# Transposes of gelu rows, normalised rows and ternary weights by DMA instead of TensorE

## The chip, the core and the metric

The kernel runs on one core of a Trainium2 chip. The time is that of the device, in microseconds (us), the median of several executions. The engines are PE (TensorE), DVE (VectorE), ACT (ScalarE), POOL (GpSimd) and SP (SyncE, which here only issues DMAs).

## The reference

x has 4 batches of 256 rows and 256 columns. All is computed from the normalised rows xn:

```
xn = layernorm(x)
q = xn @ Wq.T; latent = xn @ Wkv_down.T; k = latent @ Wk_up.T; v = latent @ Wv_up.T     # 16 heads of 16
att = softmax(where(band of 64 or first 4 columns, causal; q k.T / 4))
h = gelu(bitlinear(xn, w_fc))            # 256 x 1024; bitlinear: rows normalised again, quantised in the
f = bitlinear(h, w_proj)                 # forward value, weights sign(round(w / mean|w|)) * mean|w|
out = x + (att @ v) @ Wo.T + f
```

## The kernel before

One batch is one iteration b of a loop that is written out by hand: each engine's instructions stand in their order, and semaphores join them. TensorE contracts over the partition axis, so what is contracted has to lie transposed. Three things are transposed by PE into PSUM, as matmuls with an identity: the normalised rows (`transposed_rows`, L978), the gelu rows (`hidden_transposed`, L1126, 128x128 fp32 blocks, eight per tile i of 128 rows) and the ternary weights, fp16 (`first_ternary` L961, `second_ternary` L968). What is contracted in more than fp16's precision is split into a high and a low fp16 half: ACT writes the high half from PSUM (`rows_high` L453, `hidden_high` L461), DVE the low one, value less high half (`rows_low` L706, `hidden_low` L780). The two halves `gh` and `glo` are the stationary operands of `second_product` (L1136), which multiplies them by `prT`, the transposed ternary w_proj.

Most products go to a ring of three PSUM tiles of two banks each. `ORDER` lists who takes the next tile and what has to be done before it is free; `take` waits for that. Two more banks, `aux` and `acc`, are used by name: `acc` holds the second product, then the attention's numerator of half the heads, then the output product.

Iteration b works on three batches: attention scores and values of b, projections and row maxima of f = b + 1, the second product of a = b - 1. PE's order in b = 1 is: `maxima_transposed` (L1082), `hidden_transposed`(a, 1), `sink_scores` (L1093, L1097), `window_scores` 0 (L1107 to L1117), `second_product`(a, 0), `window_scores` 1, `latents`(f) (L990), `second_product`(a, 1), `window_scores` 2 and 3, `q_products` (L1004), `k_products` (L1019), `values` 0, `v_products`, `window_maxima` 0 (L1057, L1063), `values` 1, `window_maxima` 1, `fc_tile`(b, 0) (L1072), `window_maxima` 2, `fc_tile`(b, 1), `window_maxima` 3, `transposed_rows`(b + 2), `output_product` (L1172), `hidden_transposed`(b, 0). In b = 2 the two `fc_tile`s of the last batch stand in the place of `transposed_rows`. Iteration 0 computes the thresholds of the ternary weights (`weight_means` L649 to L661) and turns them.

On ACT stand the exponentials (L475), the gelu (`hidden`, L447), the copies from PSUM and `table_ahead` (L526), which loads the table of the next function. DVE has the row maxima (L748), reciprocals (L786), low halves and the statistics of the hidden rows (`hidden_stats`, L771, L775) and of the next rows (`row_stats` L689, `row_norm` L701). POOL computes the factors of the rows and adds the residual. SP loads `xres` (L279) and stores the result (L282, L285).

## Time and profile before

| | |
|---|---|
| median of 3 runs | 146.12 us (145.68 to 147.16) |
| profiled execution | 145.57 us, span 143.0 us |
| PE, DVE, ACT, POOL busy | 134.5, 101.1, 86.1, 29.7 us |
| HBM read, written | 6.23 MB, 1.05 MB |

The span is the time from the first to the last recorded instruction of the core; the execution's own time is longer. Busy is the union of an engine's instructions. A matmul's duration includes its way through the array, so neighbours overlap: the time that a piece of PE's work costs is read from the chain, in which each piece ends where the next begins.

### The profile page before, as it was taken

How to read it: one execution, taken by the hardware profiler on the slowest of the kernel's cores; microseconds unless marked ns; L12 is line 12 of the kernel's file. 1: busy time of each engine (PE TensorE's matmuls, PEld its weight loads, DVE VectorE, ACT ScalarE, POOL GpSimd, SP SyncE). 2: the span in 40 equal slices, each digit the busy share in tenths (PEclk: the TensorE clock that was granted, in tenths of full speed). 3: DMA queues.
4: the chain of work that ended last, by engine and by line, in shares of the span. 5: the costliest groups of instructions: out<-in, count | busy, mean ns of one | idle time of the engine just before them, and what ended most of it. 6: DMA issues, size and time to landing. Idle time of an engine off the chain costs nothing.

```text
span 143.0 us, 5152 instructions
## 1 busy us (share of the span) xinstructions
PE 134.5 (94%) x2264; PEld 103.8 (73%) x2264; DVE 101.1 (71%) x188; ACT 86.1 (60%) x128; POOL 29.7 (21%) x65
## 2 busy tenths in 40 slices
PE   7787799899999989999999999999999999999991
PEld 7575566789875477888875488888764477898981
DVE  0559999866999984952696979601969806963992
ACT  2499699498543599347542697457073479659020
POOL 8770510003500000049300000317000000025500
PEclk9999999999999999999999999999999999999999
DMA  3999720200000003000310000000400000000222
GB/s 119 309 318 371 190 72 0 77 3 7 0 5 5 0 0 78 0 5 0 95 61 0 5 0 0 7 5 0 151 5 0 0 2 5 0 5 0 76 75 73
DMA packets 7985, 7.59 MB, mean 53 GB/s; under 512 B 2580, under 2 KB 7608, under 8 KB 7864
## 3 DMA queue, kind: packets, MB, share of 16 engines
q1 hardware_dynamic: 6524, 5.90, 13.8%
q10 hardware_dynamic: 1440, 1.38, 3.2%
q8 instruction: 17, 0.28, 0.8%
q14 instruction: 4, 0.03, 0.1%
HBM read 6.23 MB, written 1.05 MB: 51 GB/s over the span
## 4 chain that ended last, share of the span: by engine, by line
PE 62%; DVE 10%; issue 1%; POOL 1%; DVEq 0%
PE acc L1136 8%; PE ring L1072 8%; PE ring L1126 5%; PE ring L1117 5%; PE acc L1162 4%; PE aux L1162 4%; PE ring L1004 4%; PE ring L1109 3%; PE acc L1172 3%; PE ring L1057 3%; PE ring L1136 3%; DVE mx L748 2%; DVE rden L786 2%; PE acc L1154 2%; PE ring L1063 2%; PE aux L1097 2%
## 5 line engine op out<-in xcount | busy, mean ns | idle before, releaser
L475 ACT ACTIVATE E<-ring,un 128x1024 f32<-128x1024 f32 x16 | 17.8, 1115 | 12.8 <-PE ring L1117 12.7
L748 DVE TENSOR_REDUCE mx<-ring 128x8 f32<-128x1024 f32 x16 | 19.4, 1220 | 2.8 <-PE ring L1063 2.6
L335 POOL TENSOR_SCALAR veh<-mvh 128x2 f32<-128x2 f32 x4 | 0.9, 218 | 71.6 <-DVE mvh L775 71.5
L447 ACT ACTIVATE gl<-ring,a 128x1024 f32<-128x1024 f32 x8 | 8.9, 1111 | 10.9 <-PE ring L1072 10.9
L780 DVE SCALAR_TENSOR_TENSOR glo<-ring,gam_r,gh 128x1024 f16<-128x1024 f32 x8 | 10.1, 1264 | 5.5 <-ACT gh L461 5.5
L716 DVE SCALAR_TENSOR_TENSOR Q<-qh,rowlo,ring 128x1024 f16<-128x1024 f16 x4 | 5.1, 1280 | 9.8 <-ACT qh L488 9.7
L1004 PE MATMUL ring<-xhT,wqT 128*128 128x256 f16 x64 | 10.3, 273 | 0.8 <-DVE wqT L624 0.8
L1136 PE MATMUL acc<-prT,gh 128*128 128x256 f16 x48 | 10.8, 274 | 0.0
L1136 PE MATMUL acc<-prT,glo 128*128 128x256 f16 x48 | 10.8, 272 | 0.0
L771 DVE BATCH_NORM_STATS2 sth<-gl 128x6 f32<-128x512 f32 x16 | 10.1, 675 | 0.0
L498 ACT ACTIVATE V<-ring 128x768 f32<-128x768 f32 x4 | 3.2, 811 | 10.7 <-PE ring L1045 10.7
L1117 PE MATMUL ring<-Q,KH 32*128 32x64 f16 (+1 forms) x192 | 9.6, 199 | 0.0
L1072 PE MATMUL ring<-fcT,xhT 128*128 128x512 f16 x32 | 9.6, 381 | 0.0
L1057 PE MATMUL ring<-mask,idb 128*128 128x512 bf16 x32 | 9.6, 380 | 0.0
L1072 PE MATMUL ring<-fcT,xlT 128*128 128x512 f16 x32 | 9.5, 379 | 0.0
L1109 PE MATMUL ring<-mov,bias 100*128 100x192 bf16 x64 | 9.3, 246 | 0.0
L1117 PE MATMUL ring<-Q,KL 32*128 32x64 f16 (+1 forms) x192 | 9.0, 197 | 0.0
L461 ACT ACTIVATE gh<-ring,gam_r 128x1024 f16<-128x1024 f32 x8 | 8.8, 1120 | 0.3 <-PE ring L1126 0.2
L1117 PEld LDWEIGHTS ring<-Q,KH 32*128 32x128 f16 x192 | 7.7, 93 | 1.7
L1063 PEld LDWEIGHTS ring<-KH,Q 32*64 32x64 f16 (+1 forms) x192 | 3.8, 100 | 6.8 <-issue 6.8
L1126 PE MATMUL ring<-idf,gl 128*128 128x128 f32 x64 | 8.6, 277 | 0.0
L1107 PE MATMUL ring<-mov,bias 100*128 100x64 bf16 x64 | 8.5, 194 | 0.0
(199 smaller groups left out, 366.9 us busy)
## 6 DMA issues: line engine op xcount, KB each, us to landing
wfc_r<-in_L_ffn_w_fc SPq DMA_DIRECT2D x1, 1024.0 KB, 6.9
wpr_r<-in_L_ffn_w_proj SPq DMA_DIRECT2D x1, 1024.0 KB, 7.4
xres<-in_L_attn_x SPq DMA_DIRECT2D x4, 256.0 KB, 4.0
bias<-in_c_bias SPq DMA_DIRECT2D x1, 825.0 KB
xin<-in_L_attn_x ACTq DMA_DIRECT2D x3, 256.0 KB, 3.2
out<-ob SPq DMA_DIRECT2D x3, 256.0 KB, 3.4
xin<-in_L_attn_x SPq DMA_DIRECT2D x1, 256.0 KB, 3.4
wq_r<-in_L_attn_Wq ACTq DMA_DIRECT2D x1, 256.0 KB, 3.8
```

The lines of the kernel that those rows point to most:

```text
L475: nc.scalar.activation(E[:, 2 * gp:2 * gp + 2, 2 * tp:2 * tp + 2, :].rearrange("p g t q -> p g (t q)"), slot("p2", b, r)[:], ACT.Exp, scal ...
L748: nc.vector.tensor_reduce(out=mx[:, i, 8 * gp:8 * gp + 8], in_=slot("f_p1", f, r)[:].rearrange("p a (t k) -> p (a t) k", t=NT), axis=AX.X, ...
L771: nc.vector.bn_stats(sth[:, i, j, :], gl[:, b % 2, i, 512 * j:512 * j + 512]).then_inc(sth_ok[0], 1)
L780: nc.vector.scalar_tensor_tensor(out=glo[:, i].rearrange("p k n -> p (k n)"), in0=flat(slot("t2T", b, i)), scalar=gam_r[:, 0:1], in1=gh[:, ...
L1004: last = nc.tensor.matmul(s[:, t // 2, (t % 2) * T:(t % 2 + 1) * T], wqT[:, w_half, c, G * t:G * t + G].rearrange("p h d e -> p (h d e)"), ...
L1057: nc.tensor.matmul(s[:, a, :].rearrange("p (t k) -> p t k", t=NT), idb[:], (mask0, mask1)[i][:].unsqueeze(1).to_broadcast([P, NT, P]), sta ...
L1072: last = nc.tensor.matmul(s[:, n, :], src[:, b % 2, c, i * P:(i + 1) * P], fcT[:, c, 512 * n:512 * n + 512], start=(m == 0), stop=(m == 2 ...
L1109: nc.tensor.matmul(s[:, a, T * j + BLK:T * j + T], bias[:, H + hm, :], mov[:, BLK:T], start=False, stop=False, skip_group_check=True)
L1117: last = nc.tensor.matmul(s[:, a, T * j + q0:T * j + q0 + n], K[g:g + 32, t, k0:k0 + P], Q[g:g + 32, t, q0:q0 + n], start=False, stop=True ...
L1126: last = nc.tensor.transpose(s[:, k // 4, (k % 4) * P:(k % 4 + 1) * P], gl[:, b % 2, i, k * P:(k + 1) * P], idf[:])
L1136: last = nc.tensor.matmul(o, src[:, i, k, :], prT[:, k, :], start=((i == 0 or b == B - 1) and k == 0 and src is gh), stop=(k == FC - 1 and ...
L1162: last = nc.tensor.matmul((acc, aux)[c][32 * k:32 * k + 32, part * T + q0:part * T + q0 + m], w.rearrange("p a d -> p (a d)"), E[:, g, t, ...
```

## The change

The three transposes leave PE, but for the rows of batch 0. A DMA transpose takes fp16 alone, so the halves are now split before they are turned: ACT and DVE write `xh`, `xl`, `gh` and `glo` from SBUF in the row layout, and SP issues `dma_start_transpose` for each: two per half of the normalised rows, one per half of a gelu tile, one per weight. PE waits for their semaphores: `xT_ok` in `latents`, `gT_ok` in `second_product`, `fcT_ok` and `prT_ok`. `hidden_high`(b, 0) follows its gelu at once. The rows are turned two iterations ahead, so `xhT` and `xlT` have three buffers. The layouts of `fcT` and `prT` follow what the DMA writes, and the moving operand of their products has two or four pieces of 128 columns. `second_product` moves behind `window_scores` 2 and 3; `latents`(f) moves to the iteration's start and from `aux` to the ring, in iteration 0 behind `window_scores` 3; `values` 1 moves behind `window_maxima` 1. On DVE `latents_low`(1) stands behind `second_ternary`, and `latents_low`(f) ahead of `hidden_low`. On POOL `second_scale` comes after the row factors. `xres` and `out` are issued behind the transposes.

```diff
--- before.py
+++ after.py
...
-        fcT = sb("fcT", [P, CC, F], fp16)
-        prT = sb("prT", [P, FC, C], fp16)
+        fcT = sb("fcT", [P, FC, CC, P], fp16)
+        prT = sb("prT", [P, CC, FC, P], fp16)
...
+        xh = sb("xh", [P, TT_, C], fp16)
+        xl = sb("xl", [P, TT_, C], fp16)
+        xhT = sb("xhT", [P, 3, CC, T], fp16)
+        xlT = sb("xlT", [P, 3, CC, T], fp16)
...
+            ORDER += [("lat", f, 0, [(latl_ok, f, 2)])] if 0 < b and f < B else []
+            ORDER += score_slots(b, range(4))
+            if f < B:
+                ORDER += projection_slots(f) + maxima_slot(f, 0) + maxima_slot(f, 1) + maxima_slot(f, 2)
+                ORDER += fc_slot(b, 0) + maxima_slot(f, 3) + fc_slot(b, 1)
+                ORDER += fc_slot(f, 0) + fc_slot(f, 1) if f == B - 1 else []
...
+            def rows_turned(n):
+                wait(sp, mm_q, n - 3)
+                wait(sp, fc, n - 3)
+                for ok, src, dst in ((xh_ok, xh, xhT), (xl_ok, xl, xlT)):
+                    wait(sp, ok, n - 1)
+                    for i in range(TT_):
+                        sp.dma_start_transpose(dst[:, n % 3, :, i * P:(i + 1) * P], src[:, i, :]).then_inc(xT_ok[0], 16)
+            def hidden_turned(b, i):
+                wait(sp, pr, b - 1, i + 1)
+                wait(sp, gh_ok, b, i + 1)
+                sp.dma_start_transpose(ghT[:, i], gh[:, i, :]).then_inc(gT_ok[i][0], 16)
+                wait(sp, glo_ok, b, i + 1)
+                sp.dma_start_transpose(gloT[:, i], glo[:, i, :]).then_inc(gT_ok[i][0], 16)
+            def first_turned():
+                sp.wait_ge(w_tern, 1)
+                sp.dma_start_transpose(fcT[:].rearrange("p k c n -> p (k c) n"), tern[:, 0]).then_inc(fcT_ok, 16)
+            def second_turned():
+                sp.wait_ge(w_tern, 1 + CC)
+                sp.dma_start_transpose(prT[:].rearrange("p c k n -> p (c k) n"), tern[:, 1]).then_inc(prT_ok, 16)
             for b in range(B):
+                if b:
+                    hidden_turned(b - 1, 0)
+                    hidden_turned(b - 1, 1)
+                else:
+                    first_turned()
+                    rows_turned(1)
+                    second_turned()
+                if b + 2 < B:
+                    rows_turned(b + 2)
+                if b == B - 1:
+                    hidden_turned(b, 0)
+                    hidden_turned(b, 1)
                 wait(sp, xa_ok, b - 1)
                 sp.dma_start(xres[:], x_v[b]).then_inc(ld_res[0], 16)
-                if b + 1 < B:
-                    wait(sp, o_ok, b)
-                    sp.dma_start(out_v[b], ob[:]).then_inc(st_out[0], 16)
+                if b:
+                    wait(sp, o_ok, b - 1)
+                    sp.dma_start(out_v[b - 1], ob[:]).then_inc(st_out[0], 16)
...
+                if b:
+                    second_scale(b - 1)
...
+            def rows_high(n):
+                wait(act, xn_ok, n)
+                wait(act, xT_ok, n - 2)
+                nc.scalar.activation(xh[:], xn[:], ACT.Copy).then_inc(xh_ok[0], 1)
...
+                wait(act, gT_ok[i], b - 1)
+                nc.scalar.activation(gh[:, i, :], gl[:, b % 2, i, :], ACT.Copy, scale=gam_r[:, 0:1]).then_inc(gh_ok[0], 1)
...
-                if b:
-                    hidden_high(a, 1)
+                if 0 < b and f < B:
+                    latents_high(f)
...
                 exponentials(b, 1)
-                if 0 < b and f < B:
-                    latents_high(f)
                 exponentials(b, 2)
-                if b == 0:
-                    latents_high(1)
+                if 0 < b and b + 2 < B:
+                    rows_high(b + 2)
...
                     hidden_high(b, 0)
+                exponentials(b, 3)
                 if b:
                     ffn_scaled(a, 0)
                     ffn_scaled(a, 1)
-                exponentials(b, 3)
                 if f < B:
                     if b == 0:
-                        first_transposed()
+                        latents_high(1)
+                        rows_high(2)
                     queries_high(f)
...
                     attended_high(b, 0)
+                    attended_high(b, 1)
                     hidden(b, 0)
-                    attended_high(b, 1)
+                    hidden_high(b, 0)
                     hidden(b, 1)
...
-                    if b + 2 < B:
-                        table_ahead(b, ACT.Exp)
-                        rows_high(b + 2)
-                    if b == 0:
-                        second_transposed()
+                    table_ahead(b, ACT.Exp)
                     attended(b)
-                    hidden_high(b, 0)
-                    if f == B - 1:
-                        table_ahead(b, ACT.Exp)
+                    hidden_high(b, 1)
...
                 wait(dve, gh_ok, b, i + 1)
-                nc.vector.scalar_tensor_tensor(out=glo[:, i].rearrange("p k n -> p (k n)"), in0=flat(slot("t2T", b, i)), scalar=gam_r[:, 0:1],
-                                               in1=gh[:, i].rearrange("p k n -> p (k n)"), op0=ALU.mult, op1=ALU.subtract).then_inc(glo_ok[0], 1)
+                wait(dve, gT_ok[i], b - 1)
+                nc.vector.scalar_tensor_tensor(out=glo[:, i, :], in0=gl[:, b % 2, i, :], scalar=gam_r[:, 0:1],
+                                               in1=gh[:, i, :], op0=ALU.mult, op1=ALU.subtract).then_inc(glo_ok[0], 1)
...
-                if 0 < b and f < B:
-                    rows_low(f)
                 maxima_moved(b)
                 if b:
+                    if f < B:
+                        latents_low(f)
                     hidden_low(a, 0)
+                    if b + 2 < B:
+                        row_stats(b + 2)
+                    hidden_low(a, 1)
+                    if b + 2 < B:
+                        row_norm(b + 2)
                     hidden_stats(a, 0)
-                    hidden_low(a, 1)
                     hidden_stats(a, 1)
+                    if b + 2 < B:
+                        rows_low(b + 2)
                 else:
                     row_norm(1)
                     weight_means(0)
                     first_ternary()
                     rows_low(1)
                     weight_means(1)
-                if f < B:
-                    latents_low(f)
-                if b + 2 < B:
-                    row_stats(b + 2)
-                    row_norm(b + 2)
-                if b == 0:
+                    row_stats(2)
+                    row_norm(2)
                     second_ternary()
+                    latents_low(1)
+                    rows_low(2)
...
+                wait(pe, xT_ok, f - 1)
+                if f == 1:
+                    wait(pe, exs, 0)
+                o = take("lat", f)[:, 0, 0:T] if f > 1 else aux[:, 0:T]
...
-            def hidden_transposed(b, i):
-                s = take("t2T", b, i)
-                wait(pe, gelu, b, i + 1)
-                for k in range(FC):
-                    last = nc.tensor.transpose(s[:, k // 4, (k % 4) * P:(k % 4 + 1) * P], gl[:, b % 2, i, k * P:(k + 1) * P], idf[:])
-                last.then_inc(tr_h[0], 1)
...
+                wait(pe, gT_ok[i], b)
+                pe.wait_ge(prT_ok, 16)
...
-                    for src in (gh, glo):
-                        last = nc.tensor.matmul(o, src[:, i, k, :], prT[:, k, :], start=((i == 0 or b == B - 1) and k == 0 and src is gh),
-                                                stop=(k == FC - 1 and src is glo), skip_group_check=True)
+                    for src in (ghT, gloT):
+                        last = nc.tensor.matmul(o.rearrange("p (c n) -> p c n", n=P), src[:, i, k, :], prT[:, :, k, :],
...
-                if b:
-                    hidden_transposed(a, 1)
+                if 0 < b and f < B:
+                    latents(f)
                 sink_scores(b)
                 window_scores(b, 0)
+                if b == 0:
+                    weight_totals(1)
+                window_scores(b, 1)
+                window_scores(b, 2)
                 if b:
                     second_product(a, 0, acc[:, 0:C])
-                else:
-                    transposed_rows(1)
-                    weight_totals(1)
-                window_scores(b, 1)
+                window_scores(b, 3)
                 if b:
-                    if f < B:
-                        latents(f)
                     second_product(a, 1, acc[:, C:2 * C])
-                window_scores(b, 2)
-                if b == 0:
-                    latents(1)
                 if f < B:
-                    window_scores(b, 3)
                     if b == 0:
-                        first_ternary()
+                        latents(1)
                     q_products(f)
                     k_products(f)
                     values(b, 0)
                     v_products(f)
                     window_maxima(f, 0)
+                    window_maxima(f, 1)
                     values(b, 1)
-                    window_maxima(f, 1)
+                    window_maxima(f, 2)
                     fc_tile(b, 0)
-                    window_maxima(f, 2)
+                    window_maxima(f, 3)
                     fc_tile(b, 1)
-                    window_maxima(f, 3)
-                    if b + 2 < B:
-                        transposed_rows(b + 2)
-                    else:
+                    if f == B - 1:
                         fc_tile(f, 0)
-                    if b == 0:
-                        second_ternary()
-                    if f == B - 1:
                         fc_tile(f, 1)
                     output_product(b)
-                    hidden_transposed(b, 0)
                 else:
-                    hidden_transposed(b, 0)
...
```

How the instructions stand at three places that the prediction speaks of. PE, from the end of iteration 0 into iteration 1, before (L1172 is `output_product`, L1126 `hidden_transposed`, L1082 `maxima_transposed`, L1093 and L1097 the first part of `sink_scores`):

```order
L1172 MATMUL acc<-woT,yhT 128x256 x4
L1172 MATMUL acc<-woT,ylT 128x256 x2
L1126 MATMUL ring<-idf,gl 128x128 x8
L1082 MATMUL aux<-idb,mhl 32x128 x2
L1126 MATMUL ring<-idf,gl 128x128 x8
L1093 MATMUL aux<-mov,bias 64x256 x2
L1097 MATMUL aux<-Q,BDH 64x256 x2
```

and now, with the line numbers of the changed kernel (L1180, L1097, then L1005 `latents`):

```order
L1180 MATMUL acc<-woT,yhT 128x256 x4
L1180 MATMUL acc<-woT,ylT 128x256 x2
L1097 MATMUL aux<-idb,mhl 32x128 x2
L1005 MATMUL ring<-xhT,wkvT 128x256 x4
L1005 MATMUL ring<-xlT,wkvT 128x256 x2
L1108 MATMUL aux<-mov,bias 64x256 x2
L1112 MATMUL aux<-Q,BDH 64x256 x2
```

The sixteen transposes round `maxima_transposed` are gone, and the six matmuls of `latents` stand where eight of them stood.

SP in one iteration, before and then now (from the `xres` of iteration 0 to the store of batch 0):

```order
L282 DMA out<-ob 128x2x256
L279 DMA xres<-in_L_attn_x 128x2x256
```

```order
L313 DMA xres<-in_L_attn_x 128x2x256
L287 DMA_TRANSPOSE ghT<-gh 128x8x128
L289 DMA_TRANSPOSE gloT<-glo 128x8x128
L287 DMA_TRANSPOSE ghT<-gh 128x8x128
L289 DMA_TRANSPOSE gloT<-glo 128x8x128
L281 DMA_TRANSPOSE xhT<-xh 128x2x128 x2
L281 DMA_TRANSPOSE xlT<-xl 128x2x128 x2
L313 DMA xres<-in_L_attn_x 128x2x256
L316 DMA out<-ob 128x2x256
```

Four transposes of gelu halves and four of the next rows now stand in one queue, and `xres` behind them; the second gelu tile's high half stands behind the first one's low half.

DVE at the start of iteration 1, before and then now (L765/L792 `maxima_moved`, L780/L808 `hidden_low`, L771/L798 `hidden_stats`, L711/L738 `latents_low`, L707 `row_stats`, L722 `row_norm`, L733 `rows_low`):

```order
L706 TENSOR_TENSOR xlT<-ring,xhT 128x512
L765 COPY mov<-aux 32x256
L780 SCALAR_TENSOR_TENSOR glo<-ring,gam_r,gh 128x1024
L771 BN_STATS sth<-gl 128x6 x2
L775 BN_AGGR mvh<-sth 128x2
L780 SCALAR_TENSOR_TENSOR glo<-ring,gam_r,gh 128x1024
L771 BN_STATS sth<-gl 128x6 x2
L775 BN_AGGR mvh<-sth 128x2
L711 TENSOR_TENSOR lat<-aux,lat 64x256
L712 TENSOR_TENSOR latS<-aux,latS 64x64
```

```order
L792 COPY mov<-aux 32x256
L738 TENSOR_TENSOR lat<-ring,lat 64x256
L739 TENSOR_TENSOR latS<-ring,latS 64x64
L808 SCALAR_TENSOR_TENSOR glo<-gl,gam_r,gh 128x1024
L707 BN_STATS st<-xin 128x6 x2
L711 BN_AGGR mv<-st 128x2 x2
L808 SCALAR_TENSOR_TENSOR glo<-gl,gam_r,gh 128x1024
L722 TENSOR_SCALAR xn<-xin,mv,rs 128x256 x2
L798 BN_STATS sth<-gl 128x6 x2
L802 BN_AGGR mvh<-sth 128x2
```

`latents_low` moved from behind both gelu tiles to ahead of them, and the work on the rows of batch 3 moved in between and behind.

## Rows read from the trace of the kernel before

**Rows 1.** The page's head, its part 1 and the granted clock of part 2.
```profile
span 143.0 us, 5152 instructions
PE 134.5 (94%) x2264; PEld 103.8 (73%) x2264; DVE 101.1 (71%) x188; ACT 86.1 (60%) x128; POOL 29.7 (21%) x65
...
PEclk9999999999999999999999999999999999999999
```
**Rows 2.** The chain that ended last, by time: start us, us, what; iterations 0 and 1.
```profile
53.53 0.87 PE ring L1126 x8
54.41 0.22 PE aux L1082 x2
54.62 1.02 PE ring L1126 x8
...
57.87 1.85 PE acc L1136 x16
...
65.36 2.73 PE ring L1004 x24
...
82.04 0.59 PE ring L978 x4
...
83.94 0.87 PE ring L1126 x8
84.81 0.21 PE aux L1082 x2
```
**Rows 3.** The same chain, iterations 2 and 3.
```profile
112.44 3.56 PE ring L1072 x16
...
118.19 0.21 PE aux L1082 x2
...
127.37 1.02 PE ring L1126 x8
...
130.43 0.44 PE acc L1154
```
**Rows 4.** Timeline of ACT: start us, us, engine, line, what; round an iteration's end.
```profile
65.30 0.83 ACT L514 ACTIVATE ffn<-acc,a 128x256 f32<-128x256 f32 x2
...
82.44 1.28 ACT L526 ACT_TABLE_LOAD   x1
...
84.32 0.68 ACT L519 ACTIVATE att<-acc,un 128x512 f32<-128x512 f32 x1
84.89 1.11 ACT L461 ACTIVATE gh<-ring,gam_r 128x1024 f16<-128x1024 f32 x1
```
**Rows 5.** The page's group of `hidden_low`: busy us, mean ns, idle before it.
```profile
L780 DVE SCALAR_TENSOR_TENSOR glo<-ring,gam_r,gh 128x1024 f16<-128x1024 f32 x8 | 10.1, 1264 | 5.5 <-ACT gh L461 5.5
```
**Rows 6.** Timeline of DVE in iteration 0, with the ternary weights.
```profile
27.58 2.35 DVE L667 SCALAR_TENSOR_TENSOR tern<-wfc_r,pthr,signs 128x2048 f16<-128x2048 f32 x1 [0.45 <-issue]
...
30.95 0.20 DVE L661 TENSOR_SCALAR gam<-gam 128x1 f32<-128x1 f32 x1
32.37 0.43 DVE L711 TENSOR_TENSOR lat<-aux,lat 64x256 f16<-64x256 f32 x1 [1.21 <-ACT latS L482]
...
32.97 0.75 DVE L689 BATCH_NORM_STATS2 st<-xin 128x6 f32<-128x256 f32 x2
...
38.52 0.88 DVE L682 TENSOR_SCALAR tern<-tern,tmean 128x1024 f16<-128x1024 f16 x2
```
**Rows 7.** Part 3 of the page: queue, packets, MB, share of 16 engines' span.
```profile
q1 hardware_dynamic: 6524, 5.90, 13.8%
```
**Rows 8.** The DMA view: issues, KB each, us from issue to landing.
```profile
xres<-in_L_attn_x SPq DMA_DIRECT2D x4, 256.0 KB, 4.0
...
out<-ob SPq DMA_DIRECT2D x2, 128.0 KB, 1.8
```
**Rows 9.** Timeline of SP: start us, us, what; one issue.
```profile
69.31 0.40 SPq L282 DMA_DIRECT2D out<-ob  x1
```
**Rows 10.** What PE waited for, of the longest: us in total, times, longest us.
```profile
PE ring L1004 <- DVE wqT L624: 0.8, 1, 0.8
```

More of the change, by code:

```diff
@@ L157, in layer_kernel @@
         a2 = sb("a2", [P, TT_], fp32)
-        gh = sb("gh", [P, TT_, FC, P], fp16)
-        glo = sb("glo", [P, TT_, FC, P], fp16)
+        gh = sb("gh", [P, TT_, F], fp16)
+        glo = sb("glo", [P, TT_, F], fp16)
+        ghT = sb("ghT", [P, TT_, FC, P], fp16)
+        gloT = sb("gloT", [P, TT_, FC, P], fp16)
         ring = [ctx.enter_context(nc.psum_tensor(f"ring{i}", [P, 2, 512], fp32)) for i in range(3)]
@@ L427, in weight_magnitudes @@
                                          accum_out=wsum[:, n, c:c + 1]).then_inc(w_abs[n], 1)
-            def first_transposed():
-                for c in range(CC):
-                    act.wait_ge(w_tr, 4)
-                    nc.scalar.activation(fcT[:, c, :], slot("t_fc", 0)[:, c, :].bitcast(fp16), ACT.Copy).then_inc(fcT_ok[0], 1)
-            def second_transposed():
-                for j in range(2):
-                    act.wait_ge(w_tr, 5)
-                    nc.scalar.activation(prT[:, 4 * j:4 * j + 4, :], slot("t_pr", 0)[:, j, :].bitcast(fp16).rearrange("p (k c) -> p k c", k=4),
-                                         ACT.Copy).then_inc(prT_ok[0], 1)
             def hidden(b, i):
@@ L949, in weight_totals @@
                 nc.tensor.matmul(acc[:, n * N_SUM:(n + 1) * N_SUM], ones[:], wsum[:, n, :], start=True, stop=True).then_inc(w_tot, 1)
-            def first_ternary():
-                s = take("t_fc", 0)
-                pe.wait_ge(w_tern, 1)
-                for c in range(CC):
-                    for k in range(FC):
-                        last = nc.tensor.transpose(s[:, c, :].bitcast(fp16)[:, k * P:(k + 1) * P],
-                                                   tern[:, 0, k * C + c * P:k * C + (c + 1) * P], idh[:])
-                last.then_inc(w_tr, 1)
@@ L961, in second_ternary @@
-            def second_ternary():
-                s = take("t_pr", 0)
-                pe.wait_ge(w_tern, 1 + CC)
-                for j in range(2):
-                    for k in range(4):
-                        for c in range(CC):
-                            last = nc.tensor.transpose(s[:, j, :].bitcast(fp16)[:, k * C + c * P:k * C + (c + 1) * P],
-                                                       tern[:, 1, c * F + (4 * j + k) * P:c * F + (4 * j + k + 1) * P], idh[:])
-                last.then_inc(w_tr, 1)
@@ L1067, in fc_tile @@
             def fc_tile(b, i):
-                wait(pe, fcT_ok, 0)
+                pe.wait_ge(fcT_ok, 16)
                 s = take("fc", b, i)
```

114 lines of the change are left out of this document (49 added, 65 removed).

## The prediction

> **What bounds the kernel now.** I read the page's busy shares first, then the chain that ended last, then what PE waits for, then the timelines of ACT and DVE round the seams. PE is busy 134.5 of 143.0 us, DVE 101.1 and ACT 86.1 [rows 1]. The chain says more than the share: from the end of iteration 0 to the last product it runs on PE alone, piece against piece, and the reader is to see that iteration 1 begins at 54.4, iteration 2 at 84.8 and iteration 3 at 118.2 us [rows 2, 3]: 30.4, 33.4 and 24.8 us to the span's end. So PE's work is the time, and the transposes that the change takes from PE lie on the path: 0.87 and 1.02 us for the eight `gl` blocks of a tile, 0.59 us for the rows [rows 2]. The profiled execution took 145.57 us for a span of 143.0, so 2.6 us lie round the span; the median of the runs is 0.55 us over that execution. I add 3.1 us to a span to compare it with the median.
>
> **What PE loses.** Per iteration 0.87 + 1.02 + 0.59 = 2.5 us, in iteration 3 three tiles, 3.1 us, in iteration 0 also the two ternary weights. If nothing took their place, this would be some 10 us in all. What takes their place is a transfer: a gelu tile reaches `second_product` by gelu, `hidden_high` (ACT), `hidden_low` (DVE), SP, DMA, where before DVE's result was read at once. ACT and DVE keep their instructions in number and shape. I price `hidden_high` and `hidden_low` from SBUF at what they take from PSUM, 1.11 and 1.26 us [rows 4, 5], and ACT's four copies of the weights, gone, at nothing: ACT is no bound.
>
> **The price of a transfer** is the disputed term, since this trace has no DMA transpose. I write S for the time by which one half of a tile (128 x 1024 fp16, 256 KB) holds the queue and the DMA engines, and F for what then passes until its semaphore is full. The row blocks (64 KB) take S/4, but not under an issue, 0.40 us [rows 9]; a weight (512 KB) takes 2S.
> S from below: the SP queue's packets moved 5.90 MB in 13.8% of 16 x 143.0 us [rows 7], which is 316 us of one engine, 18.7 KB per us; 256 KB over 16 engines are 16.4 KB each, 0.9 us. S from above: the same 316 us by 6524 packets are 48 ns each; cut by 128 columns, as the result's shape 128x8x128 has it, the half is 128 x 8 = 1024 pieces, 64 per engine, 3.1 us. I take 2.0, between them: pieces of 256 B are shorter than that queue's mean packet of 0.9 KB, so 48 ns is too dear, and a transpose writes in shorter runs than a copy, so 0.9 us is too cheap. F: a store of 128 KB lands 1.8 us after its issue [rows 8]; less the 0.4 of the issue that is 1.4. Upwards, a 256 KB load from HBM lands after 4.0 us [rows 8], less 0.4 and 0.9 is 2.7. I take 1.4, because nothing here is read from HBM.
> By the Trainium skill (Advanced Engine Details and Errata, X-Bar Transpose) transposing DMAs are as fast as regular ones; then S is at its lower end, which is the second rival below. The Trainium skill (VectorE: DVE Perf Modes, The three transpose paths) speaks against the change: it gives 1309 ns for one 128x128 block by DMA and 390 ns by TensorE. If blocks followed each other at that pace, an estimate from that page is 10.5 us for a half and a kernel of some 300 us. No row here shows either.
>
> **Where the wait falls.** In iteration b, ACT first loads the exp table (1.28), then `attended` (0.6), `hidden_high` of tile 1 (1.0), an `xin` issue (some 0.5, by [rows 9]) and `latents_high` (0.5, about one DVE instruction of its size); DVE adds `latents_low` (0.6), which now stands ahead of `hidden_low` of tile 0 (1.3) [rows 4 to 6]. The gelu ends about when the iteration begins, so `glo` of tile 0 is complete 6.0 us after that. PE meanwhile has 0.2 + 0.7 + 1.1 us and three `window_scores` of 1.1 to do, with half a us of waiting for a bank, and stands at `second_product` after 5.3 to 5.9 us. So nothing covers the transfer. SP issues in the written order gh0, glo0, gh1, glo1, so gh1, ready long before, queues behind glo0 and glo1 behind gh1: tile 1 is there at 6.0 + 3S + F. After it come the second product (1.8 us, [rows 2]) and the rest of the iteration. That rest is 84.81 - 65.36 = 19.45 us before, less 0.59 and 0.87 [rows 2], and an estimated 0.4 more where `fc_tile`(b, 1) now takes the bank of the third `window_maxima`, whose reduction is behind DVE's reciprocal: 18.4 us.
> - Iteration 1: 6.0 + 3S + F + 0.1 + 1.8 + 18.4 = 26.3 + 3S + F = 33.7 us at S = 2.0, F = 1.4, against 30.4. (For S under 1.4 tile 0 decides: 29.1 + S + F.)
> - Iteration 2: no `xin` issue on ACT (-0.6), two more `fc` tiles (+3.5 of the 3.56 of [rows 3]): 29.2 + 3S + F = 36.6, against 33.4.
> - Iteration 3: `glo` of tile 0 is complete after 1.9 us, for `hidden_high` of it ran an iteration earlier and no latents stand ahead; `values` waits for `ffn_scaled` (0.83 us [rows 4] and the hops between engines, 1.15), which a transpose covered before; from `values` on it is 143.0 - 130.4 = 12.6 us [rows 3]: 1.9 + 3S + F + 0.1 + 1.8 + 1.15 + 12.6 = 17.5 + 3S + F = 24.9, against 24.8. The halves of its own two tiles queue up to 1.9 + 7S + F = 17.3 us at the least, and the last is needed at 1.9 + 3S + F + 9.7 = 19.0: in time, but late if S nears 3. The last `xres` load is behind them on SP; it is needed 3 us later still.
> - Iteration 0: `first_ternary` ends at 29.9 us [rows 6]. SP then turns fcT (2S), and behind it, by the order on its queue, the four row blocks (S), and `latents`(1) waits for those: 29.9 + 3S + F + 0.1 = 37.4, where PE stood ready at 31. With latents 0.7 and 18.4 for the rest, iteration 1 begins at 49.1 + 3S + F = 56.5, against 54.4.
>
> Sum: 56.5 + 33.7 + 36.6 + 24.9 = 151.7 us of span, 154.8 by the median: **155 us**, 9 us slower. PE would be idle for 6 us once, and for 3.5 and 1 us in each of two iterations. The `ffn`, `out` and `xres` work moves back with PE but has slack. POOL's scale of the hidden rows, now behind the next rows' factors, is asked for only after `second_product`; it costs nothing.
>
> **The rivals.**
> - **Faster**, by one mechanism: the three `window_scores` ahead of `second_product` cover the transfer. Place: the first wait on the semaphore of tile 0. With S + F near zero iteration 1 begins at 53.9, for `second_ternary` now stands ahead of `latents_low`(1) on DVE and holds `k_products`: it can start 1.8 us earlier than before (rows statistics at 31.15 for 32.97), ends at 37.6 for 39.4, then 0.6 and 15.7 us [rows 6]. The iterations are then PE's own work, 29.4 and 32.2, and 23.4: 138.9, by the median 142 us. To be 1% under the runs, S + F must be under 1.5 us. Against it: the quickest transfer in the trace, half as large, lands after 1.8. For it: PE's relief is real, and the cover may be some tenths longer than I make it. 0.10.
> - **No difference**: S = 0.9, F = 1.4, a transpose at a copy's pace. 53.9 + 31.4 + 34.3 + 23.4 = 143.0 us, to the tenth the span of before: what PE gives back, the waits take; 146 us. 0.15.
> - **The queue becomes the bound**: S = 3.1 and F = 1.4 to 2.7. Iterations 59.8, 37.0, 39.9, and 1.9 + 7S + F + 6.1 = 31.1 in the last: 167.8 to 173; 171 to 176 us. For it: many short pieces. 0.20.
> - **The clock**: the granted clock is full in every slice [rows 1], and PE's longest wait on another engine's result is 0.8 us [rows 10]; now it would stand still for 3.5 to 6 us three times. If it came back at 1.2 GHz for as long as it was idle, each time half of that is lost, 13 / 2 = 6 us: 161 us. No row prices it, so it is no part of the sum. 0.13. The Trainium skill (TensorE: Matmul & The Clock Gate, Part 1) has idleness drop the engine to the lower level; by that rule this rival happens wherever the waits are as long as I forecast.
>
> **The numbers.** The forecast itself, S between 1.3 and 2.6 at full clock, has 0.42 and spans 148 to 164. A change under 1%, 1.5 us, can't be told from none. Faster by over 1%: 0.10. Within 1%: 0.15. Slower: 0.75, the forecast, the queue and the clock. The range goes from 145, which leaves out most of the first rival, to 176, the upper end of the queue's: about 0.15 is outside.
>
> **What would show it.** In the changed profile: no PE group that reads `gl`; DMA_TRANSPOSE rows on SP's queue, whose spacing for `ghT` and `gloT` is S and whose landing less that is F; the chain passing DVE `glo`, a transfer and then PE's `prT`, twice per iteration; `latents`(1) idle for some 6 us on `xT_ok`. PE's busy time some 10 us less in a longer span. S read there under 1.3 would prove the size wrong, with the formulas standing; iterations 1 and 2 shorter than 30 us with S over 1.5 would prove the mechanism wrong, for then the transfers are covered by something that I did not see.

## The result, and the profile after

The changed kernel takes 160.31 us (median of 4 runs, 159.59 to 161.24) against 145.9 us of the kernel before: a ratio of 1.098, 95% interval 1.088 to 1.109. The profiled execution has a span of 158.9 us, 15.9 more than before. In this ratio and those below, executions more than 1.5% above the fastest of their kernel are left out, in the medians they are not (five of combo_two's twelve, two of combo_late's ten, one of combo's ten).

The page's head, part 1, the granted clock by slice and the SP queue's row of part 3, to be read beside [rows 1] and [rows 7]:

```profile
span 158.9 us, 4966 instructions
PE 132.4 (83%) x2156; PEld 98.0 (62%) x2156; DVE 101.1 (64%) x188; ACT 82.4 (52%) x124; POOL 32.6 (20%) x65
...
PEclk9999999975599999956999999858999999999999
...
q1 hardware_dynamic: 30892, 11.90, 34.3%
```

TensorE has less to do, stands still for longer, and works at half clock in three places. Where the 15.9 us are shows in a cut by iteration (first `maxima_transposed` to the next; columns: stretch, its length, busy time and instructions of PE, granted clock, DMA share, GB/s). First the kernel before, then the changed one:

```profile
24.70:54.30 29.60, 28.43 (x539) 1.00 0.04 12
54.30:84.70 30.40, 30.40 (x543) 1.00 0.10 28
84.70:118.10 33.40, 33.40 (x555) 1.00 0.06 18
118.10:143.00 24.90, 22.03 (x449) 1.00 0.10 34
```
```profile
25.10:60.50 35.40, 27.25 (x491) 0.86 0.32 66
60.50:94.80 34.30, 30.73 (x522) 0.90 0.28 63
94.80:132.70 37.90, 34.20 (x540) 0.91 0.21 47
132.70:158.90 26.20, 19.52 (x425) 1.00 0.61 102
```

The iterations grew by 5.8, 3.9, 4.5 and 1.3 us. PE's idle time (length less busy) went from 4.0 to 22.1 us; its busy time fell by 2.6, although about 7.2 us of the new busy time are only the half clock (worked out below). At full clock it would have fallen by 9.8, the "some 10 us" of the forecast.

The chain that ended last (start us, us, what), which answers to [rows 2, 3]:

```profile
27.99 2.36 DVE tern L685
30.36 1.60 SPq L293
32.02 1.96 SPq L281
34.02 1.25 SPq L281
35.31 1.24 SPq L281
36.60 2.34 DMA xlT<-xl
38.98 1.46 PE aux L1005 x6
40.45 4.33 PE ring L1019 x24
...
64.60 1.30 DVE glo L808
65.91 3.24 DMA gloT<-glo
69.20 3.59 PE acc L1143 x16
...
72.85 0.16 PE ring L1124
...
73.64 0.97 PE ring L1132 x24
74.61 1.85 PE acc L1143 x16
```

In iteration 0 the chain now passes through the ternary weights on DVE, four issues on SP's queue and a transfer; in each later iteration, where it had been PE alone, it passes through DVE's `glo` and a transfer (and, over a wait of 0.4 or 0.5 us, through DVE's row maxima). The same `q_products` take 4.33 us for 2.73 [rows 2], the same product 3.59 for 1.85: half clock behind each wait. `latents`(1) takes 1.46 for 0.76 (its piece at full clock in the run combo). Behind the product come the scores, 0.97 for 0.56 (in iteration 2 0.91), and ahead of them four pairs of matmuls that take 0.85 us for 0.45; one matmul of such a pair in the kernel before:

```profile
59.75 0.08 PE ring L1109
```

This makes 2.3 + 2.55 + 2.5 = 7.4 us by the pieces. The run combo_two, with the same instructions on PE at full clock, has it busy for 104.5 us where the changed kernel has 111.7: 7.2 us. What PE waited for (total, times, longest):

```profile
PE acc L1143 <- DMA gloT<-glo: 7.5, 3, 3.2
...
PE aux L1005 <- DMA xlT<-xl: 7.1, 1, 7.1
```

The chain above has the issues of iteration 0 on SP's queue: L293 turns 512 KB, L281 64 KB each. Here those of 256 KB, beside the plain one of [rows 9], and the DMA view of 65 to 70 us (times issued, us from issue to landing):

```profile
65.91 1.23 SPq L289 DMA_TRANSPOSE gloT<-glo  x1
67.19 1.32 SPq L287 DMA_TRANSPOSE ghT<-gh  x1
68.56 1.34 SPq L289 DMA_TRANSPOSE gloT<-glo  x1
```
```profile
gloT<-glo SPq DMA_TRANSPOSE x2, 3.2
ghT<-gh SPq DMA_TRANSPOSE x1, 3.4
```

An issue holds the queue for 1.2 to 2.0 us in these rows whether it moves 64 or 256 KB; a plain one takes 0.40 [rows 9]. Each of the three halves lands 3.2 to 3.4 us after its issue, at 69.1, 70.6 and 71.8 us, so they follow each other at 1.2 to 1.5 us, the pace of the issues.

### The profile page after: what moved, and what is told of

Read it like the earlier page. It is cut to its first block, busy times and chain, and to the rows that moved or that the text cites. A ratio compares the mean times of both kernels' runs of the same rounds, so it can differ in the third digit from the quotient of the medians.

```text
span 158.9 us, 4966 instructions
## 1 busy us (share of the span) xinstructions
PE 132.4 (83%) x2156; PEld 98.0 (62%) x2156; DVE 101.1 (64%) x188; ACT 82.4 (52%) x124; POOL 32.6 (20%) x65
## 3 DMA queue, kind: packets, MB, share of 16 engines
q1 hardware_dynamic: 30892, 11.90, 34.3%
## 4 chain that ended last, share of the span: by engine, by line
PE 45%; DVE 21%; DMA 11%; issue 7%; SPq 6%; ACT 5%; POOL 2%; DVEq 0%; ACTq 0%
PE acc L1143 8%; DVE mx L775 7%; DMA gloT<-glo 7%; PE ring L1019 6%; PE ring L1087 6%; PE acc L1170 5%; DVE rden L814 3%; SPq L281 3%; PE acc L1162 3%; DVE glo L808 2%; DMA idf<-in_c_idf 2%; PE ring L1143 2%; PE ring L1034 2%; ACT V L522 2%; DVE tern L685 1%
## 5 line engine op out<-in xcount | busy, mean ns | idle before, releaser
L499 ACT ACTIVATE E<-ring,un 128x1024 f32<-128x1024 f32 x16 | 17.0, 1123 | 13.0 <-PE ring L1132 13.0
L1143 PE MATMUL acc<-prT,ghT 128*128 128x256 f16 x48 | 13.9, 322 | 7.6 <-DMA gloT<-glo 7.5
L775 DVE TENSOR_REDUCE mx<-ring 128x8 f32<-128x1024 f32 x16 | 19.2, 1217 | 0.5 <-PE ring L1078 0.4
L1143 PE MATMUL acc<-prT,gloT 128*128 128x256 f16 x48 | 13.9, 322 | 0.0
L1019 PE MATMUL ring<-xhT,wqT 128*128 128x256 f16 x64 | 11.5, 297 | 1.0 <-DVE wqT L642 1.0
L808 DVE SCALAR_TENSOR_TENSOR glo<-gl,gam_r,gh 128x1024 f16<-128x1024 f32 x8 | 10.2, 1285 | 2.9 <-ACT gh L486 2.8
L530 ACT ACTIVATE yhT<-y 128x256 f16<-128x256 f32 x8 | 3.3, 410 | 15.7 <-DVE y L819 15.7
L1143 PEld LDWEIGHTS acc<-prT,ghT 128*128 128x128 f16 x48 | 5.4, 113 | 9.4 <-DMA gloT<-glo 8.0
L343 POOL TENSOR_SCALAR ve<-mv 128x2 f32<-128x2 f32 x4 | 1.8, 458 | 40.9 <-DVE mv L711 40.9
L798 DVE BATCH_NORM_STATS2 sth<-gl 128x6 f32<-128x512 f32 x16 | 10.0, 667 | 0.0
L1122 PE MATMUL ring<-mov,bias 100*128 100x64 bf16 x64 | 9.3, 203 | 0.0
L486 ACT ACTIVATE gh<-gl,gam_r 128x1024 f16<-128x1024 f32 x8 | 9.2, 1146 | 0.1
```

What stands on the lines that cost most here:

```text
L486: nc.scalar.activation(gh[:, i, :], gl[:, b % 2, i, :], ACT.Copy, scale=gam_r[:, 0:1]).then_inc(gh_ok[0], 1)
L499: nc.scalar.activation(E[:, 2 * gp:2 * gp + 2, 2 * tp:2 * tp + 2, :].rearrange("p g t q -> p g (t q)"), slot("p2", b, r)[:], ACT.Exp, scal ...
L775: nc.vector.tensor_reduce(out=mx[:, i, 8 * gp:8 * gp + 8], in_=slot("f_p1", f, r)[:].rearrange("p a (t k) -> p (a t) k", t=NT), axis=AX.X, ...
L798: nc.vector.bn_stats(sth[:, i, j, :], gl[:, b % 2, i, 512 * j:512 * j + 512]).then_inc(sth_ok[0], 1)
L808: nc.vector.scalar_tensor_tensor(out=glo[:, i, :], in0=gl[:, b % 2, i, :], scalar=gam_r[:, 0:1], in1=gh[:, i, :], op0=ALU.mult, op1=ALU.su ...
L1019: last = nc.tensor.matmul(s[:, t // 2, (t % 2) * T:(t % 2 + 1) * T], wqT[:, w_half, c, G * t:G * t + G].rearrange("p h d e -> p (h d e)"), ...
```

## The experiments

Each was run beside the kernel before. Theory at their start: PE waits for transfers that start late and lie behind others on one queue, and half the clock goes with each long wait. Rivals: the clock alone, the bandwidth, VectorE as the new bound. Length of the iterations in us, from the same cut, and the time:

| run | 0 | 1 | 2 | 3 | median us | ratio to before (95%) |
|---|---|---|---|---|---|---|
| before | 29.6 | 30.4 | 33.4 | 24.9 | 145.9 | 1 |
| changed | 35.4 | 34.3 | 37.9 | 26.2 | 160.31 | 1.098 |
| warm | 35.3 | 33.2 | 35.6 | 27.5 | 159.32 | 1.092 (1.085-1.099) |
| late_product | 35.8 | 30.3 | 33.8 | 26.1 | 152.55 | 1.048 (1.042-1.054) |
| rows_first | 32.0 | 34.0 | 37.6 | 26.4 | 156.91 | 1.077 (1.072-1.083) |
| untransposed | 35.2 | 30.6 | 32.2 | 26.0 | 150.91 | 1.039 (1.032-1.046) |
| low_first | 35.8 | 29.7 | 32.6 | 26.3 | 151.77 | 1.040 (1.032-1.048) |
| one_dma | 32.5 | 34.0 | 37.7 | 26.4 | 158.42 | 1.086 (1.080-1.093) |
| combo | 31.4 | 29.7 | 32.4 | 26.3 | 146.58 | 1.007 (1.003-1.011) |
| combo_two | 29.0 | 29.3 | 32.9 | 26.2 | 145.31 | 0.990 (0.985-0.995) |
| combo_late | 29.0 | 30.5 | 34.0 | 25.4 | 146.65 | 1.005 (1.001-1.009) |
| ternary_only | 28.7 | 30.4 | 33.4 | 25.3 | 144.66 | 0.994 (0.990-0.998) |

The lengths are of one execution each; iteration 0 begins between 24.5 and 26.0 us, and that is in the medians. Each ratio is to the executions of the kernel before that ran beside the run, with medians of 145.6 to 145.9 us. combo_two and combo_late have the same instructions in the last iteration, and its lengths are 26.2 and 25.4: a length can be off by that much.

**warm: the clock held by other work.**

```diff
+                if 0 < b < B - 1:
+                    wait(pe, att_ok, b - 1)
+                    kept_busy(7, acc)
                 if b:
                     second_product(a, 0, acc[:, 0:C])
...
+                        wait(pe, exs, 0)
+                        kept_busy(15, aux)
                         latents(1)
```

> The changed kernel, with matmuls of the constant ones among themselves put on TensorE while it waits: 15 ahead of latents(1), 7 ahead of second_product(a, 0) in iterations 1 and 2 (their result is overwritten). Nothing else moves; every wait for a transposed half stays. Theory: the three stretches that the profile after shows at a granted clock of 0.5, 4.6 us (39.0 to 43.6), 5.4 us (69.2 to 74.6) and 5.3 us (103.5 to 108.8), cost half of their length each, 2.3 + 2.7 + 2.65 = 7.6 us, and an engine that has something to do in the wait keeps its clock: about 152.7 us, and a granted clock of 0.97 or more. Rival: the work behind the waits is bound by VectorE's and ScalarE's steps, so a faster TensorE only waits again: 160 us, the stretches at full clock all the same. In between (156 us) if only some of the three count.

It gave back 1 us by the median. Its chain in iterations 1, 2 and 3, and PE's timeline in iteration 0:

```profile
69.29 4.90 DMA gloT<-glo
74.24 1.92 PE acc L1143 x16
...
102.96 3.20 DMA gloT<-glo
106.21 1.92 PE acc L1143 x16
...
132.03 4.67 DMA gloT<-glo
136.75 3.46 PE acc L1143 x16
```
```profile
32.78 3.62 PE L947 MATMUL aux<-ones 128*128 128x128 f32 x30
40.40 0.61 PE L1005 MATMUL aux<-xhT,wkvT 128*128 128x256 f16 x4 [4.01 <-DMA xlT<-xl]
```

In iterations 1 and 2 the matmuls of the first product are back at 272 ns (in the changed kernel they took up to 421). Iteration 2 then gives back 2.3 us, nearly all of the 2.5 that the clock had taken. Iteration 1 gives back only 1.1: the last half, which landed 3.2 us after its issue in the changed kernel, takes 4.90 here, and PE waits 1.4 us for it. In iteration 3, to which nothing was added, the first half takes 4.67 instead of 3.2, PE waits 1.5 us for it, its clock falls, and the iteration is 1.3 us longer. In iteration 0 the ones were too few: 3.6 us of work, then 4.0 of idleness, and the clock fell all the same. So the half clock is part of the loss, but with the transfers where they stand a late one takes back what the clock gives: this speaks against both pure stories. Why some halves land late is open. Of the 160 transposes of gelu halves in the ten traces that have them, 105 land 3.0 to 3.4 us after their issue, the rest after 3.6 to 5.1.

**late_product: other work ahead of the product.** In iterations 1 and 2:

```diff
+                    k_products(f)
+                    if b:
+                        second_product(a, 0, acc[:, 0:C])
+                        second_product(a, 1, acc[:, C:2 * C])
+                        v_products(f)
                     values(b, 0)
```

> The changed kernel, with second_product(a, 0) and (a, 1) of iterations 1 and 2 moved behind q_products(f) and k_products(f), v_products(f) put between them and values(b, 0), and ffn_scaled on ScalarE moved behind keys_high(f). Theory: the work moved ahead (window_scores(b, 3), q_products, k_products: about 5 us) covers the 3.2 us from the issue of gloT to its landing, so both waits of 3.2 us go, and with them the half clock behind them (2.7 us each): 160.3 - 6.4 - 5.3 = 148.6 us, and the chain no longer names gloT in iterations 1 and 2. Rival: VectorE, whose queries, keys and maxima come earlier but whose hidden_low and hidden_stats lie ahead of them, sets the pace of iterations 1 and 2: only the waits or less come back, 154 us or more.

It gave 7.8 us, between theory and rival: 4.0 and 4.1 us of the 3.9 and 4.5 by which the two iterations had grown. The waits for `gloT` fell from 7.5 to 1.6 us; in their place PE waits 3.5 us for VectorE's `mx` (1.3 in the changed kernel).

**low_first: the transfer started earlier.**

```diff
                 if b:
+                    hidden_low(a, 0)
                     if f < B:
                         latents_low(f)
-                    hidden_low(a, 0)
```

> The changed kernel, with hidden_low(a, 0) ahead of latents_low(f) on VectorE in iterations 1 to 3. VectorE waits 2.8 us per iteration for latS there, with the half that the transfer wants queued behind it, so glo of tile 0 would be complete 2.8 us earlier and land as much earlier, 0.4 us after TensorE has come to it. Theory (the late start of the transfer is the cost, not its length): waits of 3.2 us become 0.4, the clock does not fall: 160.3 - 2 x 2.8 - 5.3 = 149.4 us. Rival (as the two runs with the clock held and with the product moved suggest): the second half's transfer, issued 2.6 us behind the first on the same queue, is then waited for; it gives back about 4 us in each of the two iterations and no more: 152.3 us. Rival 2: k_products, which want latents_low, become late: 156 us or more.

8.5 us for one moved line (the first rival's size): iterations 1 and 2 are at 29.7 and 32.6, under the kernel before, with every transfer still in its place. What made the transfer costly there was that its input stood 2.8 us behind a wait for something else. The work on PE covers nearly all of the transfer once it starts that much earlier: of the two waits of 3.2 us 0.8 and 0.4 are left, and the clock stays full.

**untransposed: no wait at all.**

```diff
-                wait(pe, gT_ok[i], b)
+                wait(pe, glo_ok, b, i + 1)
...
-                    for src in (ghT, gloT):
+                    for src in (gh, glo):
```

Besides, `hidden_high` now waits until the product of the iteration before has read `gh`. The product reads the halves unturned, so its result is not the reference's; all transposes are still issued.

> The changed kernel, with second_product reading the untransposed halves gh and glo as soon as VectorE has written glo (so the second FFN product is not the reference's); every transpose is still issued and moves its bytes, only nothing waits for those of the hidden rows. The waits for rows 1 to 3 stay. Theory (the wait is the cost, and the clock that it takes along): 160.3 - 3.2 - 3.2 - 1.1 (the third wait, in the last iteration) - 5.3 (half clock in iterations 1 and 2) = 147.5 us. Rival 1 (the clock costs nothing): 152.8 us. Rival 2 (the transfers themselves disturb the engines, by bandwidth or a shared port, so that DVE, ACT and PE operations beside them are longer): 155 us or more, with longer operations in the stretches 66 to 76 and 100 to 110 us.

150.91, not 147.5. Iteration 2 gave 5.7 of 5.9 us, iteration 1 only 3.7, the last 0.2 of 1.1. In iteration 1 PE then waits for others (total, times, longest; 60 to 91 us):

```profile
PE acc L1163 <- ACT ffn L539: 1.3, 1, 1.3
PE ring L1088 <- DVE mx L776: 1.0, 1, 1.0
```

The second rival is seen in one place only: a `glo` of the last iteration takes 1.92 us, the others of this run 1.24 to 1.28. On the whole the transfers do not lengthen what runs beside them: in the changed kernel `mx` takes 1217 ns and the exponentials 1123, before 1220 and 1115, and VectorE is busy for 101.1 us in both. And since low_first, with its waits kept, is within 1 us of it, little more was to be had from the hidden rows.

**rows_first and one_dma: the queue in iteration 0.**

```diff
-                    first_turned()
                     rows_turned(1)
+                    first_turned()
```
```diff
-                    for i in range(TT_):
-                        sp.dma_start_transpose(dst[:, n % 3, :, i * P:(i + 1) * P], src[:, i, :]).then_inc(xT_ok[0], 16)
+                    sp.dma_start_transpose(dst[:, n % 3].rearrange("p i c t -> p (i c) t"), flat(src)).then_inc(xT_ok[0], 16)
```

> The changed kernel, with the four row-block transposes of rows 1 issued ahead of the transpose of the first ternary weights on SyncE's queue; the data are ready at 30.1 (xh) and 30.9 us (xl). Theory: an issue holds the queue for 1.2 to 1.6 us whatever its size, so the second xlT is issued at 34.6 instead of 36.6 us, lands near 36.9 instead of 38.9, and latents(1) and all behind it start 2.0 us earlier: 158.3 us. Rival: the size counts and the 512 KB of fcT, now behind, share the engines with the row blocks (or ScalarE's and VectorE's halves are what is late): 160.3 us. Nothing here takes the half clock away.

> The changed kernel, with xhT and xlT laid out by row block, so that one transpose of 128 KB turns both blocks of a half: two issues for rows instead of four, the same bytes. Theory (an issue holds the queue about 1.25 us whatever its size): the last of rows 1 is issued 2.5 us earlier and, if 128 KB land 2.4 to 3.2 us after their issue, is there 1.7 to 2.5 us earlier: about 158.2 us. Rival (the issue goes by the size, 64 KB in 1.25 us, 128 KB in 2.5 us): 160.3 us, issues of 2.5 us.

rows_first gave 3.4 us, more than the 2.0: its four issues take 1.25 each, `latents`(1) starts 2.6 us earlier in the iteration, and with the shorter wait `q_products` lose less (3.55 us for 4.33). one_dma gave 1.9 by the median, its theory (iteration 0 of its fastest execution, the profiled one, is 2.9 shorter). Its queue and wait, 128 KB per issue:

```profile
31.92 1.97 SPq L280 DMA_TRANSPOSE xhT<-xh  x1
33.94 1.26 SPq L280 DMA_TRANSPOSE xlT<-xl  x1
```
```profile
PE aux L1004 <- DMA xlT<-xl: 4.7, 1, 4.7
```

Twice the bytes in the same 1.26 us: at these sizes the issue is paid by the instruction. The first one, behind the 512 KB of `fcT`, takes 1.97, as it did with half the bytes (1.96).

**combo, combo_two, combo_late: all starts brought forward.** combo is low_first, rows_first and one_dma with `rows_high`(1) ahead of `sink_exponentials`(0) and `rows_low`(1) ahead of `first_ternary`; combo_two adds:

```diff
+                if f == B:
+                    hidden_low(a, 0)
                 maxima_moved(b)
                 if b:
+                    if f < B:
+                        hidden_low(a, 0)
+                    hidden_low(a, 1)
                     if f < B:
                         latents_low(f)
...
-                    second_ternary()
                     latents_low(1)
+                    second_ternary()
...
                 else:
+                    hidden_low(b, 0)
                     hidden_stats(b, 0)
                     hidden_stats(b, 1)
-                    hidden_low(b, 0)
```

> The changed kernel with four edits that bring transfers forward and no work moved on TensorE: hidden_low(a, 0) ahead of latents_low(f); rows 1 ahead of the ternary weights on SyncE's queue; one transpose per half of the rows; rows_high(1) ahead of sink_exponentials(0) on ScalarE and rows_low(1) ahead of first_ternary on VectorE. xl of rows 1 is then ready near 28.1 us, its transfer issued by 28.7 and landed by 32, when TensorE comes to latents(1) (31.8): iteration 0 loses its wait of 7.1 us and its 2.3 us of half clock, iterations 1 and 2 what the run of the first edit alone gives (8 to 11 us). Theory (late starts are all there is to it): 160.3 - 9.4 - 8 = 143 us, below both kernels. Rival (the queue's own pace and the transfers' 3 to 5 us remain in the way): 148 us.

> The kernel of the run combo with three more moves on VectorE: latents_low(1) ahead of second_ternary in iteration 0; hidden_low(a, 1) ahead of latents_low and row_stats, and in the last iteration hidden_low(a, 0) ahead of maxima_moved (VectorE idles 4.9 us there with its input ready); hidden_low(b, 0) ahead of hidden_stats in the last iteration. In combo TensorE stood 3.7 us before k_products(1) (the profile calls it issue; VectorE wrote the low half of lat at 38.3 us, when TensorE went on), and waited 2.3 us for gloT in all. Theory (every one of these is a late start behind unrelated work on an engine in order): 3.7 us in iteration 0, about 1 us in each of iterations 1 and 2, 1 to 2 in the last: 146.6 - 3.7 - 3.5 = 139.4 us. Rival (VectorE's own 30 us of steps per iteration set the pace as soon as the waits go): only the 3.7 us come back, 142.9 us.

> The same, with second_product of iterations 1 and 2 behind q_products and k_products too (the edit of the run late_product). Theory (the transfers still end last): the waits for gloT in iterations 1 and 2 go altogether, 1 us less than combo_two. Rival (they are covered already, and the product now stands between the keys and values(b, 0), on which VectorE waits): 1 to 2 us more than combo_two.

combo took 146.58, between its theory (143) and its rival (148): PE no longer waits for `xlT`, and stands instead 3.7 us before `k_products`(1), for VectorE, which turns to `latents_low` only at 38.32 (chain of combo, then VectorE's timeline):

```profile
32.67 2.62 PE ring L1018 x24
35.30 3.69 issue
38.99 1.03 PE ring L1033 x8
```
```profile
37.41 0.88 DVE L699 TENSOR_SCALAR tern<-tern,tmean 128x1024 f16<-128x1024 f16 x2
38.32 0.43 DVE L737 TENSOR_TENSOR lat<-aux,lat 64x256 f16<-64x256 f32 x1
```

combo_two removed that and is the fastest of the changed kind, but far from my 139.4, and over the rival's 142.9. Its median, 145.31, is only 0.3 us under the 145.6 of the kernel before beside it, so the 1.0% of the ratio is not shown as a gain. Its cut by iteration (busy times of PE, PE's weight loads, DVE, ACT, POOL, then as above) and its waits say why:

```profile
26.00:55.00 29.00, 25.07 (x492) 17.98 (x493) 25.19 (x55) 15.62 (x23) 3.75 (x8) 1.00 0.53 82
55.00:84.30 29.30, 28.19 (x522) 20.80 (x521) 21.91 (x37) 17.78 (x25) 6.66 (x12) 1.00 0.40 73
84.30:117.20 32.90, 31.75 (x539) 22.43 (x539) 20.88 (x31) 19.52 (x26) 4.01 (x6) 1.00 0.29 62
117.20:143.40 26.20, 19.45 (x425) 16.43 (x424) 16.55 (x26) 11.25 (x15) 6.92 (x8) 0.99 0.57 92
```
```profile
PE ring L1089 <- DVE mx L774: 3.2, 4, 2.1
...
PE acc L1145 <- DMA gloT<-glo: 1.1, 1, 1.1
```

PE (first busy column) is busy for 9.8 us less than before (104.5 for 114.3), but only 0.9 us of the four lengths came of it (117.4 for 118.3). Its idle time in iterations 0 to 2 is 6.2 us for 1.2, most of it for VectorE (maxima 3.2, other results 2.9), and in the last 6.8 for 2.9, of which 1.1 is a transfer and 1.4 a stop in its last product that the profile puts down to nothing. combo_late's rival was right: with the transfers covered, moving the product only costs (1.3 us; the waits for the maxima grow from 3.2 to 5.2).

**ternary_only: the one transfer that is covered.** The kernel before with

```diff
+            sp.wait_ge(w_tern, 1)
+            sp.dma_start_transpose(fcT[:].rearrange("p k c n -> p (k c) n"), tern[:, 0]).then_inc(fcT_ok, 16)
+            sp.wait_ge(w_tern, 1 + CC)
+            sp.dma_start_transpose(prT[:].rearrange("p c k n -> p (c k) n"), tern[:, 1]).then_inc(prT_ok, 16)
```

and the weights' transposes, copies and banks gone.

> The kernel before, with the two ternary weights alone turned by DMA (the changed kernel's fcT and prT, their two ring slots, 32 TensorE transposes and 4 ScalarE copies gone; hidden rows and normalised rows stay on TensorE). Nothing waits for the queue there, and fcT, prT are wanted 10 us or more after they are ready. Theory (transposes off TensorE pay where their transfer is covered): TensorE's chain loses 0.87 + 0.85 = 1.7 us, and what waited for ScalarE's 1.9 us copy behind it: 143.5 to 144.3 us, against 145.9. Rival (TensorE only waits longer for VectorE's maxima in iteration 0): 145.9 us.

144.66 us, 0.994 (0.990 to 0.998): a gain of about 1 us, 0.9 of it in iteration 0, less than the 1.6 to 2.4 of the theory.

## Why the prediction held, and where its steps were off

- **What bounds, and what PE loses:** right. 9.8 us at full clock for "some 10".
- **Where the wait falls:** right. `glo` of tile 0 is complete 65.90 - 60.5 = 5.4 us after iteration 1 begins (forecast 6.0), PE stands there just then, nothing covers the transfer, and `gh1` queues behind `glo0`. `hidden_high` and `hidden_low` take 1.15 and 1.29 us from SBUF (priced at 1.11 and 1.26). low_first shows that this late start was nearly the whole loss of iterations 1 and 2.
- **The price of a transfer:** mis-sized, by two errors of opposite sign. A half holds the queue for 1.3 us, and halves in a row land 1.2 to 1.5 us apart, where S was 2.0. What then passes until it has landed is 3.24 - 1.3 = 1.9 us, where F was 1.4. The sum for one half came near: 3.2 for S + F = 3.4. The bound of 48 ns per piece of 256 B was too dear by half: the queue's share rose from 13.8% of 143.0 to 34.3% of 158.9 us [rows 7], for 24368 packets more, which is 23 ns each or, by 64 pieces, 1.5 us per half. The lower bound, a copy's pace of 0.9, was too cheap. By the Trainium skill (Advanced Engine Details and Errata, X-Bar Transpose) transposing DMAs are as fast as regular ones; here they are not: issue 1.25 us for 0.40, and 1.5 us of the DMA engines for 256 KB where the same reckoning gives a copy 0.9. The Trainium skill (VectorE: DVE Perf Modes, The three transpose paths) gives 1309 ns for one block by DMA; that is not the pace of blocks in a row, which by 1.5 us for eight is 0.19 us.
- **Iteration 0, the term mis-sized:** the row blocks were priced by size, S/4 = 0.5 us each; each holds the queue 1.24 to 1.96. `latents`(1) came at 38.98 for 37.4, although fcT took 1.60 for 4.0 us; then 2.3 us of half clock, and iteration 1 began at 60.5 for 56.5.
- **Iterations 1 and 2:** 34.3 and 37.9 for 33.7 and 36.6. The forecast took the branch in which tile 1 decides; with S at 1.3 it is the other, in which tile 0 does, and in fact PE waits for tile 0 alone. By that branch iteration 1 is 29.1 + 3.24 = 32.3 us at full clock, 34.9 with the 2.55 of half clock, and 34.3 less the 0.6 by which `glo` came earlier than forecast. The forecast came near by errors that cancel, which is luck: a spacing too long, by 1.4 and 1.3 us, and a clock left out, 2.55 and 2.5.
- **Iteration 3:** 26.2 for 24.9. That tile 1 was there after 9.2 us, as forecast (9.3), is luck too: the halves were issued 1.3 us apart instead of 2.0, and the last landed 4.65 us after its issue instead of 3.2. PE waited 1.2 us for it, and stood 1.2 us more within its last product, where the forecast had its own halves in time. The profile doesn't say what it stood for there; the two halves of the last tile land 5.0 and 4.3 us after their issues, at 150.9 and 151.6, and PE goes on at 151.2. In combo_two the two stops are 1.1 and 1.4 us. No edit of the changed kernel brought this iteration under 25.4, and untransposed, which waits for none of these halves, has 26.0: most of its growth stays open.
- **The rivals:** the clock's came true together with the forecast, and cost 7.2 us of TensorE's work for the 6 that it was given; it should have been a term of the sum, as my own waits of 3.5 to 6 us called for it. The Trainium skill (TensorE: Matmul & The Clock Gate, Part 1) has it so: idleness drops the engine to the lower level, and here it did in each of the three long waits. "Faster" asked for transfers covered by `window_scores`; they were not. "No difference" asked for S = 0.9; it was 1.3. "The queue becomes the bound" did not come. The forecast's own span for S between 1.3 and 2.6 was added up wrongly: its formulas give 147 to 163 us, not 148 to 164.

155 us was 5 too low, inside the range; direction and mechanism were right. In the profiled span the miss is larger, 158.9 for 151.7: 4.0, 0.6, 1.3 and 1.3 us by iteration. It is the clock (7.4) and the row blocks (1.6), with some 3 us against them, for the spacing and for the `glo` of iteration 1, and 1.3 us in the last iteration. The time looks nearer than the span since I added 3.1 us to the span, and the median lies only 1.4 above it.

## What to carry to other kernels

Work taken off a bound engine was a gain here only where the transfer that replaces it is covered: ask first which instruction makes its input, and what stands ahead of that in order; one line moved on VectorE gave 8.5 us here, moving the product 7.8, holding the clock 1. Count DMA transposes of 64 to 256 KB by number and not by bytes, and join them. Leave room for a transfer that lands 1 to 2 us late. When the waits are gone, look at who is next: 9.8 us off TensorE were worth 0.9 us of the iterations, since TensorE then waited for VectorE, while the ternary weights alone, whose transfer nobody waits for, gave 1 us with none of the trouble.

## What the runs showed of the hardware

- A DMA transpose occupies the issuing queue mostly 1.25 us, at most 2.4, at 64, 128 and 256 KB, and 1.6 to 3.0 at 512 KB; a plain DMA mostly 0.4 to 0.6, once 1.46 right behind transposes.
- 256 KB of fp16 turned from SBUF to SBUF land 3.0 to 3.4 us after their issue in 105 of 160 cases and up to 5.1 in the rest; in a row they land 1.2 to 1.5 us apart when none is late.
- A packet of a DMA transpose, 246 bytes on average, takes 23 ns of one DMA engine.
- TensorE's granted clock went to its lower level, 1.2 GHz, in or behind waits of 3.2, 3.7, 4.0, 4.4, 4.7 and 7.1 us. The length of the wait alone does not decide: it fell behind one of 1.5 us too (warm, iteration 3: 0.50 from 137 to 139 us) and stayed full in one of 2.1 us (combo_two, iteration 0). The changed kernel round the end of its first wait (columns as for combo_two; 0.50 is the granted clock):

```profile
36.00:42.00 6.00, 3.02 (x15) 2.15 (x16) 2.80 (x8) 1.01 (x3) 0.95 (x2) 0.50 0.60 113
```
